# Shifting where TensorE's SBUF operands start in a decoder layer of split float32 matmuls

## What is computed

```python
# sublayer 1, for each sequence
qkv = x @ Wqkv.T + bqkv
q, k = elu(scale * q) + 1, elu(scale * k) + 1
y = q * cumsum(k * v) / clip(sum_d(q * cumsum(k)), EPS)
x = layernorm(x + y @ Wproj.T + bproj)
# sublayer 2: attention of channels, 4 heads, global + local
x = layernorm(x + 2 * (att_global + att_local) * wp + bp)
# sublayer 3: the sequence's expert, 512 -> 2048 -> 512
h = relu(x @ W1[top1] + b1[top1])
x = layernorm(x + h @ W2[top1] + b2[top1])
```

## Time and profile before

| | before |
|---|---|
| median of 3 runs | 2421.51 us |
| profiled execution | 2422.74 us, its span 2421.1 us |
| mean granted TensorE clock | 0.992 of 2.4 GHz |
| DMA, mean over the span | 146 GB/s |

### The profile page before, as it was taken

How to read it: one execution, slowest core, us unless ns; L and a number is a source line. 1 busy time by engine, 2 the same in 40 slices (tenths; PEclk the granted TensorE clock), 3 DMA queues, 4 the chain that set the end, 5 groups by cost and what they waited for, 6 DMA issues and landing times.

```text
span 2421.1 us, 33310 instructions
## 1 busy us (share of the span) xinstructions
PE 2370.7 (98%) x11584; PEld 1974.4 (82%) x11584; DVE 1635.2 (68%) x2721; ACT 1148.8 (47%) x1921; POOL 501.6 (21%) x516
## 2 busy tenths in 40 slices
PE   7889999999999999999999999999999999999997
PEld 5778888888888888888888888888888888888786
DVE  7867586675857758586685866758577585865543
ACT  5344454445444545455445454454445454544543
POOL 3231212122111311112111121221113111121200
PEclk9989999999999999999999999999999999999999
DMA  8153446354454534546344463544546345443341
GB/s 296 61 157 126 154 148 201 103 182 124 141 192 122 192 113 140 174 123 200 114 145 160 139 201 106 177 128 142 189 122 195 110 140 174 124 155 96 105 126 66
DMA packets 96552, 354.66 MB, mean 146 GB/s; under 512 B 11906, under 2 KB 11906, under 8 KB 86146
## 3 DMA queue, kind: packets, MB, share of 16 engines
q1 hardware_dynamic: 79490, 318.97, 37.6%
q0 software_dynamic: 16896, 33.56, 8.4%
HBM read 329.42 MB, written 23.07 MB: 146 GB/s over the span
## 4 chain that ended last, share of the span: by engine, by line
PE 93%; DVE 2%; ACT 1%; issue 1%; POOL 0%; ACTq 0%; DVEq 0%; POOLq 0%
PE acc L1138 28%; PE h_ps L1122 10%; PE h_ps L1124 9%; PE h_ps L1123 9%; PE m L979 6%; PE m L981 6%; PE m L980 6%; PE m L1019 2%; PE m L1020 2%; PE m L1021 2%; PE m L1035 2%; PE m L1094 2%; PE m L992 2%; PE m L1108 1%; PE m L1005 1%
## 5 line engine op out<-in xcount | busy, mean ns | idle before, releaser
L514 ACT ACTIVATE hid<-h_ps,b 128x512 f32<-128x512 f32 x256 | 176.4, 689 | 627.4 <-PE h_ps L1124 626.6
L1138 PE MATMUL acc<-we_hi,h_hi 128*128 128x512 f32 x1024 | 407.0, 397 | 1.6 <-DVE h_lo L853 1.6
L1122 PE MATMUL h_ps<-x2T_hi,we_hi 128*128 128x512 f32 x1024 | 406.2, 397 | 1.3 <-DVE x2T_lo L839 1.3
L853 DVE TENSOR_TENSOR h_lo<-hid,h_hi 128x512 fp32r<-128x512 f32 x256 | 214.1, 837 | 274.5 <-ACT h_hi L519 274.5
L1124 PE MATMUL h_ps<-x2T_hi,we_lo 128*128 128x512 f32 x1024 | 399.3, 390 | 0.0
L1138 PE MATMUL acc<-we_hi,h_lo 128*128 128x512 f32 x1024 | 399.1, 390 | 0.0
L1138 PE MATMUL acc<-we_lo,h_hi 128*128 128x512 f32 x1024 | 399.0, 390 | 0.0
L1123 PE MATMUL h_ps<-x2T_lo,we_hi 128*128 128x512 f32 x1024 | 398.7, 389 | 0.0
L845 DVE TENSOR_TENSOR we_lo<-raw,we_hi 128x1024 fp32r<-128x1024 f32 x256 | 319.7, 1249 | 29.5 <-ACT we_hi L504 29.5
L457 ACT ACTIVATE e_f<-m,sb_qkv,scale 128x512 f32<-128x512 f32 x120 | 93.5, 779 | 483.4 <-PE m L981 477.7
L979 PE MATMUL m<-xT_hi,wq 128*128 128x512 f32 x684 | 268.3, 392 | 8.5 <-DVE wq L632 8.2
(11 more groups left out here) (206 smaller groups left out, 3667.7 us busy)
## 6 DMA issues: line engine op xcount, KB each, us to landing
raw<-in_w SPq DMA_DIRECT2D x256, 512.0 KB, 4.1
wq<-wq_scratch SPq DMA_DIRECT2D x168, 512.0 KB, 3.3
x<-in_x_tok SPq DMA_DIRECT2D x16, 1024.0 KB, 5.5
x<-in_b_proj POOLq DMA_DIRECT2D x16, 1024.0 KB, 15.1
ctx_T<-in_ctxT SPq DMA_DIRECT2D x16, 1024.0 KB, 8.5
ctx_tok<-in_ctx_tok SPq DMA_DIRECT2D x16, 1024.0 KB, 4.8
x<-in_b POOLq DMA_DIRECT2D x16, 1024.0 KB, 11.6
out_dram<-x SPq DMA_DIRECT2D x16, 1024.0 KB, 4.8
```

Of the source, the lines that this page charges most:

```text
L514: act.activation(hid[:, f % 2, :], H_PS[:, :], ACT.Relu, bias=b1[:, b % 2, f:f + 1]).then_inc(h_done, 1)
L853: dve.tensor_tensor(h_lo[:, f % 2, :], hid[:, f % 2, :], h_hi[:, f % 2, :].bitcast(F32), ALU.subtract).then_inc(hlo_done, 1)
L1122: pe.matmul(H_PS[:, :], we_hi[:, g % NW, js], x2T_hi[:, j, :], start=(j == 0), stop=False)
L1138: last = pe.matmul(acc[t][:, :], hx[:, f % 2, ts], wx[:, g % NW, C:], start=(f == 0 and n == 0), stop=(f == FC - 1 and n == 2))
```

## The change

Eight tensors are allocated with 128 more elements (512 bytes) a row, and the kernel works on a part of each that begins some elements in: 72 for `wp_hi` and `wp_lo`, 64 for `xT_hi` and `xT_lo` (and with them `y_hi` and `y_lo`), 4 for `x2T_hi` and `x2T_lo`, 124 for `h_hi` and `h_lo`. An element has 4 bytes. `wq`, `we_hi` and `we_lo` stay where they were. Nothing else is changed: no instruction is added, removed or moved.

```diff
+        def moved(name, n, by):
+            tile = sb(name, [P, n * 512 + 128], F32R)
+            return tile[:, by:by + n * 512].rearrange("p (n e) -> p n e", n=n)
+
-        wp_hi, wp_lo = sb("wp_hi", [P, CC, C], F32R), sb("wp_lo", [P, CC, C], F32R)
+        wp_hi, wp_lo = moved("wp_hi", CC, 72), moved("wp_lo", CC, 72)
-        xT_hi, xT_lo = sb("xT_hi", [P, CC, T], F32R), sb("xT_lo", [P, CC, T], F32R)
+        xT_hi, xT_lo = moved("xT_hi", CC, 64), moved("xT_lo", CC, 64)
         y_hi, y_lo = xT_hi, xT_lo
-        x2T_hi, x2T_lo = sb("x2T_hi", [P, CC, T], F32R), sb("x2T_lo", [P, CC, T], F32R)
-        h_hi, h_lo = sb("h_hi", [P, 2, T], F32R), sb("h_lo", [P, 2, T], F32R)
+        x2T_hi, x2T_lo = moved("x2T_hi", CC, 4), moved("x2T_lo", CC, 4)
+        h_hi, h_lo = moved("h_hi", 2, 124), moved("h_lo", 2, 124)
```

## The result

The changed kernel takes 2446.5 us, the median of 4 runs (2445.3 to 2448.3), against 2421.8 for the kernel before in the same comparison: 1.0105 times, 95% interval 1.0093 to 1.0117. It is 25 us slower; the prediction had 2360 us and a gain. It is inside the stated range of 2320 to 2450 only because the range was stretched into that of rival R2 (2442 to 2460); the change of the time has the other sign than the forecast.

The account below looks back on a forecast made before the run. The prediction took PE's matmul stream, number times pitch, as the bound. From 2421.5 us it subtracted 66 for ups and downs and added 4 for waits, giving 2360 us, range 2320 to 2450.

Parts of the forecast that it names:

- R2: Ups and downs: the new 16-byte distance is worse and they don't settle; 20 to 39 us lost, 2442 to 2460, chance 0.27.
- What bounds the kernel: PE's own instruction stream: 9216 matmuls at a pitch of 226.7 ns make 2089 us of the 2421.
- Is 226.7 ns a floor?: Matmul pitch at full clock: 13.3 ns over 213.3 looks like the moving stream meeting the next weight load.
- (a) The distances: Moving operand against weights loaded meanwhile, no longer 512-byte multiples apart: ups and downs fall to 216 ns, 66 us gained.
- The upper bound of 240 ns: Highest pitch allowed for after the change, from the worst single matmul after a disturbance; 82 us lost in ups and downs.
- The same in both: Ups and downs both get a 16-byte distance, so one value, 66 us gained, was chosen for the two.
- The projections, put at nothing: Q, K, V at 256 bytes and output projection at 32: no gain taken; output projection at most 8 us.
- (b) Padding: Eight tensors get 128 more elements a row, 4 KB a partition, with no instruction added: zero cost.
- (c) The other engines: ScalarE and VectorE at shifted addresses: 16 h_lo of a sequence change by 2.7 us, hidden by PE.
- (d) Waits given back: PE's waits on other engines: start waits don't shrink, some mid-run waits appear; 4 us given back.
- R1: All matmuls: the distance is no cause and the change does nothing, 2421.5 us; chance 0.25.
- R3: All families of matmuls gain: 99 us, less 4, giving 2327 us; chance 0.15.

Follow-up runs that it names:

- The last experiment: TensorE alone, bursts without the layer: one fp32r element repeated 215.8 ns, bfloat16 every 4 bytes 225.8 ns, fp32r with one column of weights 231.1 ns a matmul.
- the ups undone: The changed kernel with the shift of x2T put back to 0, all else as in the change: 2428.6 us, 1.0033 of the kernel before.
- the sweep: TensorE alone, 128 bursts in the order of an up, moving operand shifted by 0, 4, 8 ... 508 bytes, weights unshifted: settled pitch 226.7 to 240.0 ns.

## Why the prediction was wrong, point by point

**What bounds the kernel**: right. PE's stream of matmuls is the bound, the time is their number times their pitch, and a change of pitch came through nearly whole: 24 of the 25.5 us between the two profiled executions, the rest being the stretch at the lower clock.

**"Is 226.7 ns a floor?"**: here the prediction failed first. It took the 13.3 ns over half the slow clock's 426.7 as two streams that meet, and named the weight load as the second. The last experiment divides them: 2.5 ns are a cost that bfloat16 and a repeated element pay too, 9 to 11 ns come back when bfloat16 is spread over the stretch that fp32r reads, and in the aligned kernel nothing or 1 to 2 ns is left for a load to give back. The evidence in the earlier trace rows was real, a pitch that varies with state, but it didn't say which reads. That the load starts with the stream shows only that it could be the load. At the slower clock neither part shows (426.7 ns), so that row couldn't tell them apart.

**(a) The distances**: the term of the sum that carried the forecast, 66 us gained in ups and downs at 216 ns, measured 13 + 4 us lost. 216 ns was out of reach for any shift; 128 shifts gave 226.7 to 240.0. The upper bound of 240 ns, taken from the worst single matmul, turned out to be the worst settled pitch; that is luck, since a single distance after a disturbance doesn't bound a settled one. "The same in both" was wrong as well: ups and downs share a distance, but not the place of each start, and with the ups undone the downs cost nothing on average. And 16 bytes isn't "the smallest step off": the sweep went by 4. The projections, put at nothing, cost 8 us: 4.6 in the output projection (bounded at 8 us, as a gain), 3.5 in Q, K, V.

The Trainium skill, "TensorE: Matmul & The Clock Gate", gives 215.7 ns in "Wait - 56ns, not 53.3ns?"; bfloat16 and a repeated fp32r element agree with 215.8, contiguous fp32r, at 226.7 and more, doesn't reach it. The Trainium skill's rule of two independent read ports (same page, "Step-by-step: what each phase is for") agrees with these runs as far as a full load costs a stream nothing when the stream reads one element; it doesn't cover that the weights' place moves the pitch of an fp32r stream from 226.7 to 233 ns.

**(b) Padding**: nothing, as measured. **(c) The other engines**: nothing; h_lo 836 ns against 837. **(d) Waits given back**: 4 us in the sum, and there was no gain to take back.

**R2** was the case that came about, at 0.27. Its sign in the tail held, a step over 5.44 us. Its price of 20 to 39 us fits the total of 25 in part by luck: it was meant for ups and downs, which lost 17, and the 8 us of the projections, which it had not priced, bring the sum into its range. Its mechanism holds in one half, for the ups: they don't settle, they cycle. The downs do settle in the tail. The other half, that the distance decides, doesn't. It also missed that the disturbance is handed on: of the 17.5 us that the ups' shift costs, some 6 stand in the other families.

**R1** would have been right for 256 bytes and for padding alone. **R3** fell with (a).

## What to carry to other kernels

Leave large fp32r operands at starts that are a multiple of 256 bytes, stationary and moving alike; of all the starts tried here none was faster. A few bytes off cost up to 6% in a burst, and 16 bytes everywhere 1.7% in this kernel. Before a variation in pitch is put down to two transfers that meet, take one of them away in a burst of TensorE alone: one element streamed over and over and a one-column load settle it in a single run. And charge a shift with what it does to its neighbours, not only to its own matmuls. Last, look at the granted clock before a difference in time is divided: here 3.4 us at the lower clock made 1.5 of the 25.5 us between the two profiles.

## What the runs showed of the hardware

- The settled pitch of 512-column fp32r matmuls with full weight loads lies between 226.7 and 240.0 ns and depends on both operands' starts. For the moving operand it repeats after 256 bytes; weights moved by 256 bytes were tried only in the kernel, where they changed nothing (2421.7 us). The 240.0 stand at moving starts 4 bytes past a multiple of 16.
- A stream that reads one element over and over, or contiguous bfloat16 at a multiple of 16 bytes, runs at 215.8 ns; bfloat16 an element every 4 bytes at 225.0 to 226.7, whatever its start.
- The pitch has memory: a pair of starts runs through a cycle of several distances, or settles after up to ten matmuls, and which of these it does can depend on what ran before. Downs with their weights at 240 bytes in 256 have 228.3 ns after a narrow matmul and 226.7 after settled ups.
- Why the place of a load changes the rhythm of a stream, when a full load costs nothing beside a stream of one repeated element (215.8 ns with 1 and with 128 columns), stays open.
